# Splitting the copies of rotated down-weight blocks between ScalarE and VectorE

## What is computed

```python
def _L0_ffn_ref(x, W1, W2, W3):
    up_gate = jnp.einsum('bsd,hd->bsh', x, W1)
    up_lin = jnp.einsum('bsd,hd->bsh', x, W3)
    hidden = jax.nn.silu(up_gate) * up_lin
    hidden = fwht(hidden)                     # Hadamard transform over 2048, / sqrt(2048)
    out = jnp.einsum('bsh,dh->bsd', hidden, W2)
    return out
...
x = L0_attn_x
xn = _layernorm(x, axis=-1)
x = x + _L0_attn_ref(xn, ...) + _L0_ffn_ref(xn, ...)
xn = _layernorm(x, axis=-1)
x = x + _L1_attn_ref(xn, ...) + _L1_ffn_ref(xn, ...)
return x
```

## Time and profile before

| | us |
|---|---|
| median of 3 runs | 1761.54 |
| lowest, highest | 1761.18, 1764.38 |
| the profiled execution's own time | 1764.71 |
| its span in the trace | 1762.5 |

### The profile page before, as it was taken

One profiled execution on the slowest core, in us unless ns is written; L12 is line 12 of the kernel. 1 busy time (PEld: TensorE's weight loads), 2 busy tenths in 40 slices (PEclk: granted clock), 3 DMA queues, 4 the chain that ended last, 5 costly groups with the idle time before them and its releaser, 6 DMA issues. The chain is left out here.

```text
span 1762.5 us, 22933 instructions
## 1 busy us (share of the span) xinstructions
PE 1701.5 (97%) x8366; PEld 1370.6 (78%) x8366; DVE 1031.5 (59%) x1795; ACT 735.2 (42%) x1528; POOL 251.8 (14%) x247
## 2 busy tenths in 40 slices
PE   5999999999999979989999999989999999999998
PEld 3777878778788868867777777768888888888887
DVE  4321465464524343348999999974555654655675
ACT  4521322232213322229999999982222222222221
POOL 4001200300300031110000000004144031033230
PEclk9999999999999989999999999999999999999999
DMA  7200110110100036842554445515010010012243
GB/s 291 91 12 1 60 48 19 54 41 15 54 7 25 36 105 231 296 194 64 138 137 122 120 120 166 142 31 171 1 49 24 1 48 25 0 48 57 87 134 130
DMA packets 75663, 149.60 MB, mean 85 GB/s; under 512 B 9497, under 2 KB 26521, under 8 KB 74018
## 3 DMA queue, kind: packets, MB, share of 16 engines
q1 hardware_dynamic: 75554, 148.17, 27.1%
HBM read 101.87 MB, written 46.27 MB: 84 GB/s over the span
## 5 line engine op out<-in xcount | busy, mean ns | idle before, releaser
L1504 DVE TENSOR_TENSOR pt_lo<-p_turn,pt_hi 128x512 fp32r<-128x512 f32 (+3 forms) x384 | 200.9, 551 | 18.9 <-ACT pt_hi L1479 15.0
L1497 DVE TENSOR_REDUCE row_top<-p_score 128x1 f32<-128x128 f32 (+7 forms) x256 | 189.7, 751 | 18.9 <-PE p_score L1431 18.8
L1471 ACT ACTIVATE prob<-p_score,row_top 128x128 f32<-128x128 f32 (+7 forms) x256 | 190.2, 746 | 6.2 <-DVE row_top L1497 5.5
L1479 ACT ACTIVATE pt_hi<-p_turn 128x512 fp32r<-128x512 f32 (+3 forms) x384 | 182.7, 495 | 5.6 <-PE p_turn L1442 1.6
L1442 PE MATMUL p_turn<-ident,prob 128*128 128x128 f32 x1152 | 181.6, 276 | 1.2 <-DVE pt_lo L1504 0.9
L958 DVE TENSOR_TENSOR hid<-hid,p_up 128x512 f32<-128x512 f32 x64 | 44.0, 688 | 221.3 <-PE p_up L435 205.6
L1840 DVE TENSOR_TENSOR e_hid<-e_hid,e_p_up 128x512 f32<-128x512 f32 x64 | 44.0, 688 | 202.9 <-PE e_p_up L1726 202.9
L1457 PE MATMUL p_o<-pt_hi,v 128*128 128x512 f32 (+3 forms) x384 | 148.6, 394 | 3.9 <-ACT o_both L1487 3.1
L1442 PEld LDWEIGHTS p_turn<-ident,prob 128*128 128x128 f32 x1152 | 131.9, 141 | 14.8 <-DVE pt_lo L1504 1.6
L1429 PE MATMUL p_score<-stack 128*128 128x512 f32 (+3 forms) x384 | 128.9, 391 | 10.4 <-PEq L53 7.0
L705 ACT ACTIVATE hid<-p_gate 128x512 f32<-128x512 f32 x64 | 38.3, 598 | 220.3 <-PE p_gate L435 220.2
(11 more groups left out here) (259 smaller groups left out, 3991.9 us busy)
## 6 DMA issues: line engine op xcount, KB each, us to landing
stack<-qk_parked SPq DMA_DIRECT2D x256, 128.0 KB, 4.0
raw<-in_wgu SPq DMA_DIRECT2D x64, 256.0 KB, 2.6
qk_parked<-qk SPq DMA_DIRECT2D x16, 1024.0 KB, 3.9
v_parked<-v_out SPq DMA_DIRECT2D x16, 512.0 KB, 5.9
v<-v_parked SPq DMA_DIRECT2D x8, 1024.0 KB, 9.7
o_parked<-o_both SPq DMA_DIRECT2D x64, 128.0 KB
res<-in_x SPq DMA_DIRECT2D x8, 512.0 KB
rot<-in_w2t SPq DMA_DIRECT2D x4, 1024.0 KB, 7.4
```

The lines of the kernel that those rows point to most:

```text
L1471: act.activation(prob[r // QB][:, h % 2, r % QB, 0:width_of(r)], p_score[:, r % 2, 0:width_of(r)], ACT.Exp, bias=top[:, r:r + 1], accum_ou ...
L1479: act.activation(pt_hi[:, (BL * h + j) % PT, c0:W], p_turn[:, (BL * h + j) % TB, c0:W], ACT.Copy).then_inc(rounded, 1)
L1497: dve.tensor_reduce(top[:, r:r + 1], p_score[:, r % 2, 0:width_of(r)], AX_X, ALU.max, negate=True).then_inc(topped, 1)
L1504: dve.tensor_tensor(pt_lo[:, slot, c0:W], p_turn[:, (BL * h + j) % TB, c0:W], pt_hi[:, slot, c0:W].bitcast(F32), ALU.subtract).then_inc(sp ...
```

## The change

Of each pair ACT now copies only the first block (from bank 0) and DVE the second (from bank 1). The one semaphore `rot_copied` becomes two, one per engine: PE's wait for a bank looks at the engine that empties that bank, `store_half` waits for both, and `turn_down` for the one of its bank. DVE's eight copies are put into its list by hand.

```diff
@@ semaphores
-        rot_done, rot_copied, tok_normed = sem("rot_done"), sem("rot_copied"), sem("tok_normed")
+        rot_done, tok_normed = sem("rot_done"), sem("tok_normed")
+        rot_copied = [sem("rot_copied_act"), sem("rot_copied_dve")]
@@ SP, store_half
-                sp.wait_ge(rot_copied, SR * s + SR)
+                for i in range(2):
+                    sp.wait_ge(rot_copied[i], (SR * s + SR) // 2)
@@ PE, rotate
-                        pe.wait_ge(rot_copied, n - 1)
+                        pe.wait_ge(rot_copied[i], n // 2)
@@ PE, turn_down
-                    pe.wait_ge(rot_copied, NCH)
+                    pe.wait_ge(rot_copied[c], NCH // 2)
@@ ACT, rot_copy
-                for i in range(2):
-                    m = 2 * h + i
-                    act.wait_ge(rot_done, SR * s + m + 1)
-                    act.activation(rot[s][:, m], p_out[:, i], ACT.Copy).then_inc(rot_copied, 1)
+                act.wait_ge(rot_done, SR * s + 2 * h + 1)
+                act.activation(rot[s][:, 2 * h], p_out[:, 0], ACT.Copy).then_inc(rot_copied[0], 1)
@@ DVE
+            def rot_copy(s, h):
+                dve.wait_ge(rot_done, SR * s + 2 * h + 2)
+                dve.tensor_copy(rot[s][:, 2 * h + 1], p_out[:, 1]).then_inc(rot_copied[1], 1)
...
             rsqrt(1, quarter(0), mean_neg, inv1, neg1)
+            rot_copy(0, 0)
             first_moments(1)
...
             first_moments(2)
+            rot_copy(0, 1)
             for u in range(UNITS):
...
+                    for half in halves_before(u, c, 1):
+                        rot_copy(*half)
                     product(u, c)
                     if c:
                         lo(u, c - 1)
...
+                    if c + 1 < NC:
+                        for half in halves_before(u, c + 1, 0):
+                            rot_copy(*half)
```

## The result

The changed kernel is slower: 1769.98 us median of 9 runs (1767.1 to 1772.32) against 1761.88 for the kernel before (9 runs, 1759.36 to 1764.48). The ratio is 1.004, with a 95% interval from 1.0029 to 1.005, that is 7.0 us more, between 5.1 and 8.8. The forecast was 4.2 us more, and 2.3 more than that if the clock fell in stall two. The sign and the two mechanisms are right. The size lies about where the forecast put the worse case, both delays and the fall of the clock.

A forecast was written before the change was run, and what follows sets the result against it. The prediction took PE, busy 97% of the span, to bound the kernel. Two delays of 2.3 and 1.9 us summed to 4.2, added to the 1761.54 us median for 1765.7 us, with a range of 1763.4 to 1769.0.

The forecast's parts named there:

- stall two: 52.13 to 56.06 us: PE waits 1.41 us for `x_rest`, transposes, then waits 1.27 for ScalarE's copy of pair (2,1).
- What bounds the kernel: PE, working 97% of the span; removing ScalarE's eight copies, at most 4.3 us of its work, gives nothing.
- First delay: Block 3's copy behind quarter 2's moments makes `store_half(0)`, x quarter 3's landing and PE's pair (2,0) later; cost 2.3 us.
- Second delay: VectorE's copy of pair (2,1) stands before the reciprocal, delaying it and PE's wait for `x_rest`; cost 1.9 us.
- Other copies: VectorE's copies of the remaining pairs lie in its idle time or are covered; they cost nothing.
- stall one: 34.2 to 39.82 us: PE waits 5.63 us for a copy of pair (1,1), held by x quarter 3's landing.
- the term of nothing: Stall one's slow clock, 4.6 us of half-speed work losing 2.3 us, fires in both kernels; nothing added to the sum.
- rival R1: Clock falls in stall two as well, or stays low longer in stall one; up to 2.3 us more, 1768.0 us; chance 0.15.
- the 3.57 us of the earlier trace: PE's wait for `x_rest` ending at 22.25 us, after which the clock read 1.00; taken as evidence against rival R1.
- my count of one stall on each side: On rival R1: 5.6 us of waiting brought the clock down, 3.57 us ahead of 22.25 did not.

The follow-up runs named there:

- e3: Changed kernel with VectorE's copy of pair (2,1) moved behind rsqrt(3) and that of (0,1) before quarter 2's moments; -1.4 us against the kernel before (-3.0 to +0.2).
- e2: Changed kernel with VectorE's copy of pair (0,1) moved in front of the moments of quarter 2; +2.6 us against the kernel before (1.1 to 4.2).
- e4: Changed kernel with 13 unused small matmuls filling only PE's first wait in stall two; +6.2 us against the kernel before (4.1 to 8.3).
- e1: Changed kernel with VectorE's copy of pair (2,1) moved behind rsqrt(3); +2.8 us against the kernel before (1.2 to 4.4).
- e10: Changed kernel with unused small matmuls filling PE's waits, 22 in stall one, 14 and 5 in stall two; +3.3 us against the kernel before (1.8 to 4.9).
- e5: Kernel before with ScalarE's root of quarters 2 and 3 moved behind the copies of pair (2,0); -5.1 us against the kernel before, 1758.99 us median.
- e8: Changed kernel with unused small matmuls filling PE's waits, 26 in stall one, 14 and 5 in stall two; +3.9 us against the kernel before (2.3 to 5.6).
- e9: Kernel before with unused small matmuls filling PE's waits, 12 in stall one, 5 and 5 in stall two; -2.5 us against the kernel before (-4.1 to -0.9).

## Why the prediction was right, and where it was not

**What bounds the kernel: right.** ScalarE's saving was worth nothing: e3, which keeps it without the two delays, can't be told from the kernel before.

**First delay: right.** Store 2.1 us later (forecast 2.3; the moments of quarter 2 happened to start 0.2 us earlier in this trace), landing 2.0 later, PE's start 2.0 later; nothing was absorbed. e2, which takes it away, is faster than the changed kernel by 4.4 us of ratio, with an uncertainty of 2.4 across two sessions, so this alone doesn't say that it costs more than its waiting.

**Second delay: right.** 1.9 us at the reciprocal, 1.9 in PE's wait (1.41 to 3.30). VectorE's copy took 0.66 to 0.69 us (forecast 0.65). The estimate of 658 ns that the prediction had worked out from the Trainium skill's table ("VectorE: DVE Perf Modes", the section on the TRN2 errata) agrees with the 0.66 us of the copy at 25.00. ScalarE's took 0.57 to 0.60 in the same trace.

**Other copies: right.** Behind 22 us no wait of PE appears that the kernel before had not, and the two delays and the low clock account for the 7.4 us of lag at 77.03.

**The clock: right in stall one, mis-sized in stall two.** In stall one the term of nothing held in this trace: PE worked from 41.80 to about 46.2 at the low level, 4.4 us where it had been 4.6. In stall two the clock's fall, rival R1, got a chance of 0.15 and a price of up to 2.3 us. In the traces of the changed kernel and of e2 it fell there within or at the end of the wait of 3.3 us, in e4 one wait later, and in none of the kernels whose copy (2,1) was not delayed; and in the changed kernel's trace it cost 3.6 us. The step that failed is the one that took the 3.57 us of the earlier trace rows as evidence against: one wait of that length without a fall doesn't say that the next has none. It doesn't even hold for that same wait. Ahead of PE's first gate matmul it is there in all twelve traces, 2.85 to 4.25 us long, and in ten of them the clock fell within it or at most 1 us behind it; the profile of before is one of the two where it stayed up. So the row that I leaned on was the exception.

The mean granted clock of the timed runs points the same way: 0.9860 for the changed kernel (9 runs), 0.9885, 0.9882 and 0.9877 for the kernel before in three sessions (28, 24 and 23 runs). A thousandth of 1766 us is 1.8 us, so the lower clock takes 3.0 to 4.4 us of full-speed time more, less what of it falls into waits. But it isn't stall two alone. In one session e1, whose stall two is that of before, has a mean of 0.9874, as low as e2's 0.9875, where e3 has 0.9888. The first delay alone goes with 2.6 us of lost clock by the same working; where in the execution it lies no run shows.

The rule of the Trainium skill that I had named beside R1 ("TensorE: Matmul & The Clock Gate", "Why this matters for your kernels": no idle gaps between bursts) fits stall two of this kernel better than my count of one stall on each side did. It doesn't tell one gap from another: the gaps of 3.57 us (before) and 3.86 (e10) left the clock up.

**The range:** the median came out at 1769.98, 1 us above its upper end; by the ratio, 1.004 times the 1761.54 of the runs shown at the time is 1768.6, inside it. What the forecast left out is the 2.8 us beyond the 4.2 of waiting (0.9 to 4.6 by the interval): the clock, and perhaps a transfer that is late by more than its store.

**What stays open:** how the 2.8 us beyond 4.2 divide between the clock and the landing of x. That the clock has a part in the changed kernel is shown (3.6 us in its trace, and filling gives 3.1 back in the timed runs). But filling gives 2.1 back before as well, and the filled kernels still lie 5 to 6 us apart, so how much of the difference is the clock's is not shown.

## What to carry to other kernels

Before work moves to an idle engine, ask what stands in front of it in that engine's list and what behind: here a copy of 0.7 us stood behind statistics that a transfer held up, and made a store 2.1 us late; another stood in front of a chain on which the matmul engine waited, and made it 1.9 us late. Where a store stands ahead of loads in one queue, whoever completes the stored data also sets the time of the loads; complete it as early as possible. And a wait of the matmul engine has to be priced with its clock: two waits that grew by 2 us each cost 7 together (5.1 to 8.8), and moving one wait out of a list (e5) was worth more than sharing out the work.

## What I had not expected of the hardware

- In e4 the low clock began as a wait of 1.27 us ended, though 3.1 us of the longer wait before it had been filled with small matmuls; with both waits filled (e8), the clock stayed up.
- The length of a wait alone doesn't decide: 3.57 us (before) and 3.86 (e10) left the clock up, while 2.87 (e9), 3.30 (the changed kernel) and 3.33 (e2) went with a fall. Even at one place of the list it differs: ahead of the first gate matmul 2.87 us left it up in e10, and 2.88 in the changed kernel didn't.
- The clock of the same program differs between executions: in the profile of before it was at 1.00 from 20 to 30 us, in that of the changed kernel, the same up to there but for one copy, at 0.83. Timed runs of one kernel lie some 5 us apart, more than most single effects here.
- A long stall hides this: PE came to stall one between 33.8 and 37.3 us in the traces with it and left it when the copy was done. With the stall gone (e5) the early loss counts in full: 3.5 us at pair (1,1).
